# Row maxima split and groups normalised on GpSimd in the order of entries, with the leading bf16 parts of keys and queries

## The reference

```python
x = x + _L0_xattn_ref(_layernorm(x, axis=-1), ctx_1024, ctx_1024, ...)
q = (Q @ Wq.T).reshape(B, S, H, Dk).transpose(0, 2, 1, 3)     # Q: normalised x
k = (K @ Wk.T).reshape(B, S, H, Dk).transpose(0, 2, 1, 3)     # K, V: the context
scores = jnp.einsum('bhqd,bhkd->bhqk', q, k) / jnp.sqrt(jnp.float32(Dk))
attn = jax.nn.softmax(scores, axis=-1)
ctx = jnp.einsum('bhqk,bhkd->bhqd', attn, v)
return ctx.transpose(0, 2, 1, 3).reshape(B, S, E) @ Wo.T
```

## Time and profile before

| | us |
|---|---|
| three runs | 1463.28, 1466.83, 1469.79 |
| median | 1466.83 |
| profiled execution, its time | 1466.42 |
| its span | 1464.6 |
| busy in the span: PE, DVE, ACT, POOL | 1180.8, 990.4, 666.8, 538.4 |
| the group of most busy time: DVE's row maxima, L604, 384 times | 253.5 |

### The profile page before, as it was taken

One profiled execution on the slowest core, in us unless ns is written; L12 is line 12 of the kernel. 1 busy time (PEld: TensorE's weight loads), 2 busy tenths in 40 slices (PEclk: granted clock), 3 DMA queues, 4 the chain that ended last, 5 costly groups with the idle time before them and its releaser, 6 DMA issues. The chain is left out here.

```text
span 1464.6 us, 34924 instructions
## 1 busy us (share of the span) xinstructions
PE 1180.8 (81%) x11141; PEld 925.2 (63%) x11154; DVE 990.4 (68%) x2918; ACT 666.8 (46%) x1423; POOL 538.4 (37%) x590
## 2 busy tenths in 40 slices
PE   4799994349999957789987879999799966499991
PEld 2577773338899815566663456677477756399991
DVE  4599886564533247989974678888487777766552
ACT  2467771116555403345554546766234343144440
POOL 3223303674325166534411232431121125752554
PEclk9899996559999957889998989999799977599996
DMA  7787733012233267435532177564200042133552
GB/s 187 197 206 189 186 106 130 30 53 74 86 89 109 66 153 190 118 101 150 144 84 51 43 176 174 145 162 106 87 1 0 0 152 74 53 120 106 147 143 73
DMA packets 140294, 163.33 MB, mean 112 GB/s; under 512 B 15240, under 2 KB 120734, under 8 KB 133196
## 3 DMA queue, kind: packets, MB, share of 16 engines
q1 hardware_dynamic: 131980, 145.38, 37.3%
q0 software_dynamic: 8192, 16.46, 4.1%
HBM read 111.19 MB, written 50.92 MB: 111 GB/s over the span
## 5 line engine op out<-in xcount | busy, mean ns | idle before, releaser
L604 DVE TENSOR_REDUCE A_neg_max<-A_s_bank 128x4 f32<-128x512 f32 x384 | 253.5, 687 | 54.6 <-PE A_s_bank L747 44.2
L464 ACT ACTIVATE A_probsT<-A_st_bank 128x512 f32<-128x512 f32 x384 | 222.2, 602 | 44.4 <-PE A_st_bank L760 43.2
L747 PE MATMUL A_s_bank<-A_k_stack,A_q_stack 72*128 72x128 bf16 x1536 | 159.4, 230 | 40.6 <-DVE A_neg_max L604 23.4
L760 PE MATMUL A_st_bank<-A_q_stack,A_k_stack 128*128 128x128 bf16 x1536 | 154.0, 225 | 7.2 <-DVE A_q_stack L620 6.2
L760 PEld LDWEIGHTS A_st_bank<-A_q_stack,A_k_stack 128*128 128x128 bf16 x1536 | 113.4, 104 | 53.2 <-issue 43.1
L747 PEld LDWEIGHTS A_s_bank<-A_k_stack,A_q_stack 72*128 72x128 bf16 x1536 | 107.4, 102 | 55.6 <-DVE A_neg_max L604 33.7
L772 PE MATMUL A_pv_bank<-A_probsT,A_v_pad 128*32 128x128 f32 x3072 | 128.1, 285 | 0.7 <-issue 0.7
L2065 ACT ACTIVATE E_h<-E_h_bank,w_L_b 128x256 f32<-128x256 f32 x184 | 76.5, 471 | 72.7 <-PE E_h_bank L2165 71.7
L2177 PE MATMUL E_y_bank<-E_w,E_h 128*128 x736 | 90.4, 276 | 2.2 <-ACT E_h L2065 0.9
L772 PEld LDWEIGHTS A_pv_bank<-A_probsT,A_v_pad 128*32 128x32 f32 x3072 | 74.4, 111 | 24.2 <-issue 2.6
L2165 PE MATMUL E_h_bank<-E_xT,E_w_u 128*128 128x256 f32 x368 | 88.6, 385 | 0.0
(11 more groups left out here) (369 smaller groups left out, 2652.1 us busy)
## 6 DMA issues: line engine op xcount, KB each, us to landing
A_q_stack<-q_scratch SPq DMA_DIRECT2D x48, 576.0 KB
A_k_stack<-k_scratch SPq DMA_DIRECT2D x32, 576.0 KB
q_scratch<-A_q_parts SPq DMA_DIRECT2D x48, 192.0 KB, 2.3
A_k_stack<-k_scratch SPq DMA_DIRECT2D x48, 192.0 KB
E_xe<-slots_in SPq DMA_DIRECT2D x53, 128.0 KB, 2.0
slots_out<-E_ye SPq DMA_DIRECT2D x53, 128.0 KB, 1.7
A_ctxT<-in_ctxT SPq DMA_DIRECT2D x24, 256.0 KB, 9.4
k_scratch<-A_k_parts SPq DMA_DIRECT2D x32, 192.0 KB
```

Source lines behind the costliest of these rows:

```text
L464: act.activation(probsT[n % 2][:, c * HQ:(c + 1) * HQ, :], st_bank[c % 2][:, :].rearrange("k (a q) -> k a q", a=HQ), ACT.Exp, scale=scale) ...
L604: dve.tensor_reduce(neg_max[:, c * HQ:(c + 1) * HQ], s_bank[c % 2][:, :].rearrange("q (a k) -> q a k", a=HQ), AX.X, ALU.max, negate=True). ...
L747: last = pe.matmul(s_bank[c % 2][:, a * S:(a + 1) * S], q_stack[slot][0:COMBO, h, at:at + S], k_stack[slot][0:COMBO, h, at:at + S], start= ...
L760: last = pe.matmul(dst, k_stack[slot][:, h, at:at + S], q_stack[slot][:, h, at:at + S], start=True, stop=spread)
```

## The change

- `split_max` moves from DVE to POOL, for all entries of A0 and A2 but the first two and for the entries of A1 from `POOL_FIRST` = 8 on. `neg_max` becomes two buffers, and DVE waits for the split of two entries ago before it writes one again.
- Groups from 2 on (from 4 on in A1) are normalised by POOL. With rotation they are now taken three groups ahead like the others, and their statistics in two halves.
- `split_rest` makes the leading part itself in all cases; ACT copies a projection once.
- POOL's work stands in the order of entries: the maxima, then under n % 4 = 0 the bias of the next group, 1 the keys, 2 the queries, 3 the normalisation three groups ahead. Its loop in A1 is written out.
- At the start of A0, SP issues the load of the last 16 tiles of x behind the stacks of group 1.

```diff
@@ -291,10 +291,10 @@
             prep(0)
             constants(2)
+            constants(3)
+            prep(1)
             if begin:
                 begin.load_x(sp, 2)
-            constants(3)
-            prep(1)
@@ -307,16 +307,13 @@
         def split_rest(eng, own, src, parts, rows, g, use, lead, done):
+            eng.wait_ge(prep_free, U * g + use + 1)
+            core.settle(eng)
             if rope:
-                eng.wait_ge(prep_free, U * g + use + 1)
-                core.settle(eng)
                 own.link(eng.tensor_tensor(src[:, :], src[:, :], rot_f[:, :], ALU.add))
                 core.settle(eng)
-                eng.tensor_copy(parts[:, 0, :], src[:, :]).then_inc(lead, 1)
-                eng.wait_ge(lead, g + 1)
-            else:
-                eng.wait_ge(lead, g + 1)
-                eng.wait_ge(prep_free, U * g + use + 1)
+            eng.tensor_copy(parts[:, 0, :], src[:, :]).then_inc(lead, 1)
+            eng.wait_ge(lead, g + 1)
@@ -328,6 +322,18 @@
+        def split_max(eng, own, b, n):
+
+            eng.wait_ge(max_done, 4 * (b + 1))
+            if not (isinstance(b, int) and b == 0):
+                eng.wait_ge(mt_ready, b)
+            core.settle(eng)
+            own.link(eng.tensor_copy(max_parts[:, hi:hi + NH], neg_max[n % 2][:, :]))
+            core.settle(eng)
+            eng.tensor_tensor(max_parts[:, lo:lo + NH], neg_max[n % 2][:, :], max_parts[:, hi:hi + NH], ALU.subtract)\
+                .then_inc(m_split, 1)
+            eng.wait_ge(m_split, b + 1)
@@ -420,26 +436,20 @@
+            add_bias(0)
+            normalise(4 if late else 2)
+            for b in range(POOL_FIRST, NB):
+                g = b // GB
+                if has_scores(b + 2):
+                    split_max(pool, own, b + 2, b)
+                if b % GB == 0 and exists(g + 1):
+                    add_bias(g + 1)
+                if b % GB == 1 and exists(g + 2):
+                    split_rest(pool, own, k_f, k_parts, kd, g + 2, KL, k_lead, k_split)
+                if b % GB == 2 and exists(g + 2):
+                    split_rest(pool, own, q_f, q_parts, D, g + 2, QL, q_lead, q_split)
+                if b % GB == 3 and exists(g + 3):
+                    normalise(g + 3)
@@ -481,12 +491,11 @@
-                for to, done in ((dst[:, :], lead), (parts[:, 0, :], prep_free)):
-                    if shared_kv:
-                        ins = act.activation(to, prep_bank[0:rows, :], ACT.Identity, bias=bias)
-                    else:
-                        ins = act.copy(to, prep_bank[0:rows, :])
-                    ins.then_inc(done, 1)
+                if shared_kv:
+                    ins = act.activation(dst[:, :], prep_bank[0:rows, :], ACT.Identity, bias=bias)
+                else:
+                    ins = act.copy(dst[:, :], prep_bank[0:rows, :])
+                ins.then_inc(prep_free, 1)
@@ -599,20 +608,12 @@
-            def row_max(b, c):
+            def row_max(b, n, c):
+                if c == 0 and not (isinstance(b, int) and b < 2):
+                    dve.wait_ge(m_split, b - 1)
                 dve.wait_ge(s_ready, 4 * b + c + 1)
@@ -691,28 +691,33 @@
-                    if has_scores(b + 2):
-                        split_max(b + 2)
+                    if isinstance(b, int) and b < POOL_FIRST:
+                        split_max(dve, own, b + 2, n)
                     place(1)
```

More of the change, by code:

```diff
@@ L381, in inverse_deviation, with normalise @@
                     .then_inc(rstd_done, 1)
+            def normalise(g):
+                inverse_deviation(g)
+                pool.wait_ge(rstd_done, g + 1)
+                pool.wait_ge(prep_ready, U * (g - 1) + X + 1)
+                for j in range(GB):
+                    last = pool.tensor_scalar(xn[:, j, :], core.x_tile(g * GB + j), mv[:, j, 0:1],
+                                              rstd[:, j:j + 1], ALU.subtract, ALU.mult)
+                last.then_inc(xn_done, 1)
             def add_bias(g):
@@ L555, in statistics @@
             def statistics(at, tiles=range(GB)):
+                if tiles[0] == 0 and not (isinstance(at, int) and at < 2):
+                    dve.wait_ge(xn_done, at)
                 for j in tiles:
@@ L564, in statistics, with normalise @@
                     last.then_inc(stats_done, 1)
[L566 to L574, removed]
+            def normalise(g):
+                dve.wait_ge(rstd_done, g + 1)
+                dve.wait_ge(stats_done, g + 1)
+                if g > 0:
+                    dve.wait_ge(prep_ready, U * (g - 1) + X + 1)
+                for j in range(GB):
+                    last = dve.tensor_scalar(xn[:, j, :], core.x_tile(g * GB + j), mv[:, j, 0:1],
                                              rstd[:, j:j + 1], ALU.subtract, ALU.mult)
-                if tiles[-1] == GB - 1:
-                    last.then_inc(xn_done, 1)
+                last.then_inc(xn_done, 1)
             def rotate(g, use, dst, parts, split, written, copies, lead):
@@ L660, in _ @@
                 statistics(g)
-                normalise(g, g)
+                normalise(g)
                 for use in range(U - g):
@@ L669, in _ @@
                 for c in range(4):
-                    row_max(b, c)
-                split_max(b)
+                    row_max(b, b, c)
+                split_max(dve, own, b, b)
             if spread:
                 spread_max(0, 0)
-            if NORM_AHEAD == 3:
+            if not late:
                 statistics(2)
-                normalise(2, 2)
             def late_result(i):
@@ L693, in place @@
                             dve.wait_ge(begin.x_loaded[2], 16)
-                        if at in STATISTICS and exists(ahead):
+                        if late and isinstance(it, int) and it == 0:
+                            if at == 0:
+                                statistics(n // GB + 2)
+                            elif at == 2:
+                                normalise(n // GB + 2)
+                            elif (n, at) == (7, 6):
+                                statistics(4)
+                        elif at in STATISTICS and exists(ahead):
                             statistics(ahead, STATISTICS[at])
-                        if at in NORMALISE and exists(ahead):
-                            normalise(ahead, ahead, NORMALISE[at])
                         for use, g in uses_at(at, it * 2 + n // GB):
```

55 lines of the change are left out of this document (12 added, 43 removed).

## The result

The changed kernel takes 1502.99 us (median of 4 runs, 1498.63 to 1507.53) against 1466.11 us before (1463.28 to 1469.79): a ratio of 1.0258, 95% interval 1.0237 to 1.0279. It is slower, by 37 us, where 10 us less was forecast. The profiled execution has a span of 1496.4 us.

A forecast was written before the change was run, and what follows sets the result against it. DVE and PE were both near their limit, so entries were timed between PE's maxima transposes. Start -5.2, first attention -3.0, third -5.3, second +3 gave -10.5 on 1466.4: 1456 us, range 1450 to 1462, chance 0.45.

The forecast's parts named there:

- normalising is worth 0.8 us per group: First attention: a group without DVE normalisation takes 21.32 us against 22.09, so normalising costs 0.8 us, not its busy time.
- No gain, no loss: Split of maxima on POOL: 0.76 us against 0.61, the 0.15 delay fitting in 0.35 free in entries without projection.
- +3 was forecast: Second attention: two entries lose 1.8 us, n = 1 gains 0.7; net +1.1 per group, three groups, +3 us.
- come out even: Rival: copies stretched 0.33 us in two entries of 12 groups (+8) eat first and third attention gains; 1463 us, chance 0.22.
- Leading parts: POOL makes them instead of ACT: PE's 0.33 us wait goes at n % 4 = 2, about -0.38 (third attention -0.55).
- The start: Start of first attention: x load behind group 1's stacks removes PE's 5.20 us stack wait; -5.2 us, ends 0 and -8.
- POOL is the slower hand: Rival: every maxima transpose behind POOL's queue comes later, 0.24 us in some 80 entries, +19; 1475 us, chance 0.18.
- threshold of 0.96 us: Split of maxima: slower POOL costs time once last maximum to end of split exceeds 0.61 + 0.35 us.
- The rule it was weighed with: Elementwise work belongs on VectorE, GpSimd about twice as slow with two inputs; by it the whole move would lose.

The follow-up runs named there:

- norm_pool: Kernel before with only the first and third attention's normalisation moved to POOL, behind the query parts, no maxima ahead: 1459.72 us, ratio 0.9954.
- two_mv: Changed kernel with mean and variance in two buffers, so statistics wait only for the normalisation before the last one: 1471.61 us, ratio 1.0029 to before.
- max_pool: Kernel before with only the split of the maxima moved to POOL, inverse deviation behind the key parts: 1481.65 us, ratio 1.0128.
- x_last: Kernel before with only the load of the last x tiles moved behind the stacks of group 1: 1462.44 us, ratio 0.9967.
- norm_dve: Changed kernel with normalisation back on DVE, POOL's inverse deviation behind the query parts: 1517.1 us, ratio 1.0348 to before.
- all_norm: Built from the changed kernel: maxima on DVE, all three attentions normalised on POOL, two buffers of mean and variance: 1460.69 us, ratio 0.9957 to before.

## Why the prediction was wrong

- **The wait it did not price.** The step that failed is "normalising is worth 0.8 us per group", used as the gain of taking it from DVE, with nothing on the other side. The 0.8 itself was about right where no wait answers it: norm_pool's group is 0.56 us shorter in the first attention and 0.71 in the third. The diff has a new wait in `statistics`, on the normalisation, and the order of POOL is written out; the prediction named neither what POOL would take for it nor what is queued behind. Bounds were to be had: 1.3 us for the inverse deviation and at least four operations behind the maxima of n % 4 = 3, against statistics that stand 1.7 us after that point in DVE's order. Measured: 4.6 us of work there, 12 waits of up to 3.3 us, 34.6 us in all, and two_mv gives 31 back. Behind DVE's wait stand the spread copy and, for it, PE.
- **"No gain, no loss" for the split of the maxima.** The parts of it were right: 0.197 and 0.219 us, 0.18 between them, 0.79 us from the last maximum to the end of the split (123.22 to 124.01) where 0.76 was forecast. POOL does 82 of them and not 88. The sum was wrong: max_pool costs 15 us by itself. In the second attention n % 4 = 2 and 3 take 6.83 and 6.80 there (worked out: 6.7 and 6.5), but in two of the four groups the delay goes on into n % 4 = 0, which takes 7.6 instead of 6.0, so the four lose 6.9 us where +3 was forecast. In the first and third a group loses 0.9 and 0.8, in the rows of A0 most of it by the stretched copy. That was the mechanism of the rival "come out even", priced at 0.33 us and not tied to the order.
- **Leading parts.** Right in size: 5.68 to 5.26 (forecast -0.38), 5.85 to 5.28 in the third (-0.55). Not foreseen: the later end moves the bias addition onto DVE's normalisation when nothing else changes.
- **The start.** Right in size (-5.2; x_last has -5.5, interval -1.2 to -8.7) and wrong in what would be seen: the wait for the stack didn't go but moved ahead.
- **The rivals.** "POOL is the slower hand" had the right sign. Its threshold of 0.96 us from the last maximum to the end of the split is passed in 16 of 82 entries, not in all: the median is 0.79, and where the parts stand ahead in the second attention it is 2.69 (698.06 to 700.75):

```profile
696.77 1.29 DVE L615 TENSOR_REDUCE A_neg_max<-A_s_bank 128x4 f32<-128x512 f32 x2
...
700.53 0.22 POOL L334 TENSOR_TENSOR A_max_parts<-A_neg_max,A_max_parts 128x16 bf16<-128x16 f32 x1 [0.18 <-POOL A_max_parts L332]
```

So the queue made the delay and not the hand, and the 31 us of the normalisation's wait are in no rival. The rule it was weighed with, that elementwise work belongs on VectorE (Trainium skill, GPSIMD Engine Reference, section 4.1), fits the duration: 824 ns against 367 by the groups' means, although the page's factor of about two is for operations with two inputs and a normalisation tile has one. norm_pool shows that this duration costs nothing where it's hidden. The time of the rival "come out even", 1463, isn't what its terms give: 1466.4 - 10.5 + 8 is 1463.9, and the start alone would be 1461.

## What to carry to other kernels

When work moves to another engine, write out that engine's order and, for each wait that the diff adds, the time at which each side comes to it; a wait on a single buffer is priced by where its reader stands in the queue, and not by its duration alone. Then lay the long instructions of the engine that got the work beside the other engine's SBUF copies: whether they meet is decided by the order, and here a meeting cost DVE up to 1 us, nearly the whole of POOL's subtraction. Undo one part at a time, since an undone part can make a wait of its own, as norm_dve did.

## What the runs showed of the hardware

A DVE cast of 128x16 in SBUF takes 171 ns alone and 484 on average beside POOL's subtraction, the longest 1131; a DVE subtraction of 128x16 in all_norm took 1.17 us, alone 0.17. POOL's cast of 512 columns, with one input, also stretched DVE's spread copy, to 1.10 us. POOL's normalisation tile did not (707 ns): of its four tiles the first took 2.73 us, until DVE's four copies were done, and the others 0.79, so a mean of 1272 hides that one operation waited out several of the other engine's. After a stall of PE of 2.6 us its granted clock was 0.62 over the next 3 us, and four 128-column products took 0.59 us instead of 0.39.
